# Attention on one core: six plain score units beside an off-diagonal group of steps, eleven beside a diagonal one, in place of eight beside each

## The chip, the cores and the metric

The kernel runs on one core of a Trainium2 chip. The metric is the device time of one execution in microseconds (us). Three executions of the kernel before took 1801.23, 1802.53 and 1802.96 us; their median, 1802.53 us, is the time before.

## The reference, cut to what matters

The input is 2048 tokens of 512 numbers. The layer adds three things: the input, a causal attention with 16 heads of 32, and a feed-forward of 4096 columns.

```
xn = layernorm(x)
q, k, v = split(xn @ w_qkv.T)             # 16 heads of 32
scores = where(causal, q @ k.T / sqrt(32), lowest)
probs  = softmax(scores)
attn   = (probs @ v) @ w_o.T
inter  = gelu_tanh(xn @ Wg.T) * (xn @ Wu.T)
out    = x + attn + inter @ Wd.T
```

The change touches only the attention. For a softmax in full precision each row's true maximum is subtracted, so the scores are computed twice: once plainly, to find the maxima, and once transposed, with the maximum folded into the matmul, for the exponentials.

## The kernel before, in words

`attention` works on eight pairs of heads. For each pair there are two streams.

**Steps.** A step is a chunk of 512 query columns against 128 keys, for both heads. Chunk qc has 4*qc + 4 steps, 40 in a pair. Four steps form a group (`GS = 4`): ten groups to a pair, 80 in all, of which groups 0, 2, 5 and 9 of each pair are diagonal (`DIAG`: the keys cross the causal border, and the steps are 512, 384, 256 and 128 columns wide), and groups 1, 3, 4, 6, 7 and 8 are off-diagonal. In the text k0 to k9 are these ten groups of a pair.

**Units.** A unit is one plain score matmul of 128 queries by up to 512 keys for one head (L1012, on TensorE), and the maximum of its rows by VectorE: `unit_max`, at L901, or at L897 where a part of the 512 is masked. A pair has 80 units (`NU`), 48 of full width at L901 and 32 masked ones at L897, eight each of 128, 256, 384 and 512 columns. They are numbered through all pairs, `NUNIT` = 640, and run about 58 units ahead of the steps; within a pair the narrow masked ones stand at 0 to 5, 10, 11, 14, 15, 18, 19, 28, 29, 34, 35, 40, 41, 54, 55, 62, 63, 70 and 71. When a row block is complete, VectorE joins its maxima (`join_parts`), GpSimd splits them in three bf16 parts (`split`, listed by `BATCHES`), TensorE turns them (`turn_max`, L1022, listed by `TURNS`), and ScalarE copies them beside the queries (`max_row`).

**How a group runs.** In its loop over k, TensorE issues the transposed scores of the next group's four steps (`scores_t`, L1040, eight matmuls; with `mask_t`, L1049, where the next group is diagonal). Seven eighths of the group's units stand between them (`some_units(0..6, 8)`). Then come the turns, the product with V of group k (L1066), row sums (L1083), and the last eighth of the units (`some_units(7, 8)`), called the tail below. TensorE takes all this in order. ScalarE computes the exponentials of the transposed scores (L818). They have three banks of PSUM (`ST_BUFS = 3`), so that `scores_t(x)` waits until the exponential of x-3 has been read. Plain units and turns share four banks (`S_BUFS = 4`), in the order of the list `ring`: `bank_free` makes a unit wait until VectorE has done what stood four places before it.

**Sums.** The exponentials are added up ahead of the row sums. GpSimd does most adds (L736): four of full width in an off-diagonal group, two each of 384, 256 and 128 columns in a diagonal one. In an off-diagonal group VectorE then adds the two sums of each head (`join_sums`, L956, two adds of 128x512), just before the group's last unit. `row_sums` of an off-diagonal group is run by TensorE in the next group. Only the groups without units give VectorE other adds.

**How many units a group has.** `unit_end` gives where group k's units end: eight more than the group before, until 640 are used up, which is in k2 of the last pair. `units_of(k)` is read by TensorE and VectorE alike. `BATCHES` follows from it; `TURNS` follows from the steps alone.

GpSimd's order in iteration k is: last adds of group k, first two adds of group k+1, the splits of `BATCHES[k]`, and in k3, k4, k6 and k7 of all but the first pair one product of the pair before with its reciprocal sums (`normalise`, L769).

Of the kernel before, what the change touches and what calls it, by code (L numbers as in the profile page):

```python
# [57 lines left out]
def values(nc, out, tt, xn_hi, xn_lo, wv_hi, wv_lo):  # L58

    t = slice(tt * P, (tt + 1) * P)  # L60
    for kt in range(KT):
        last = mm3(nc, out, xn_hi[:, kt, t], xn_lo[:, kt, t], wv_hi[:, kt, :], wv_lo[:, kt, :], kt == 0, kt == KT - 1)
    return last
# [285 lines left out]
def attention(nc, qk_scratch, v_scratch, sum_scratch, rsum_scratch, wo_t, wo_sb, attn_t, xn_hi, xn_lo, e_sb, wv_hi, wv_lo, p_v,  # L349
# [9 lines left out]
    GS = 4  # L359
# [2 lines left out]
    ST_BUFS = 3  # L362
    E_BUFS = 16
    S_BUFS = 4
    UNITS_GROUP = 8
    UNITS_FIRST = (20, 12)
    UNITS_AHEAD = 48
    TURN_LEAD = 1
# [5 lines left out]
    NS = len(STEPS)  # L374
# [5 lines left out]
    DIAG = [kt >= 4 * qc for qc, kt, _ in STEPS]  # L380
# [6 lines left out]
    NUNIT = PAIRS * NU  # L387
# [2 lines left out]

    BEHIND_V = {v: 5 for v in range(5, TT - 1)}
    FIRST_V = sum(BEHIND_V.values())
    TURNS_AT = TT - 3
    FIRST = FIRST_V + LEAD * 2
    unit_end, done = [], FIRST
    for k in range(NG):
        done = min(NUNIT, max(done + UNITS_GROUP, min(done + UNITS_FIRST[min(k, 1)], UNITS_GROUP * (k + 1) + UNITS_AHEAD)))
        unit_end.append(done)  # L400

    def units_of(k):
        return list(range(unit_end[k - 1] if k else FIRST, unit_end[k]))

# [3 lines left out]
    for p in range(PAIRS):  # L408
        for r in range(TC):
            last = p * NU + UNITS_TO[r]  # L410
            BATCHES[-1 if last <= FIRST else next(k for k in range(NG) if unit_end[k] >= last)].append((p, r))
            wanted = (p * NS + CHUNK_START[r] - LEAD) // GS
# [6 lines left out]

    BEFORE_TURNS = sum(count for v, count in BEHIND_V.items() if v < TURNS_AT)  # L420
    ring = list(range(BEFORE_TURNS)) + TURNS[-1] + list(range(BEFORE_TURNS, FIRST))
    for k in range(NG):
# [37 lines left out]
    with ExitStack() as ctx:  # L460
# [97 lines left out]
        def bank_st(x):  # L558
            return p_v[:, x % ST_BUFS, :] if x % ST_BUFS < V_FIRST else p_st3[:, :]
# [325 lines left out]
        def _(dve):  # L885
# [3 lines left out]
            def unit_max(n):  # L889
                a, i, b, w = UNITS[n % NU]  # L890
                part = max_part[:, a, i, b:b + 1]
                dve.wait_ge(scored, n + 1)
                if b == i // 4:
                    m = MASKED_UNITS.index(n)
                    if m >= 2:
                        dve.wait_ge(maxed, MASKED_UNITS[m - 2] + 1)
                    nc.vector.tensor_tensor_reduce(out=masked_scores[:, m % 2, 0:w], in0=p_s[:, slot[n] % S_BUFS, 0:w],  # L897
                                                   in1=score_mask[:, W - w:], scale=1.0, scalar=NO_MAX, op0=ALU.add,
                                                   op1=ALU.max, accum_out=part).then_inc(maxed, 1)
                else:  # L900
                    nc.vector.reduce_max(part, p_s[:, slot[n] % S_BUFS, 0:w], AX.X).then_inc(maxed, 1)  # L901
# [56 lines left out]

            for n in range(FIRST):
                unit_max(n)  # L960
# [33 lines left out]
        def _(pe):  # L994
# [8 lines left out]
            def scores(n):  # L1003

                p, u = divmod(n, NU)
                a, i, b, w = UNITS[u]
                if p == 0 and u < 2:
                    pe.wait_ge(first_loaded[a], 96)
                elif u < 2 if p else u in (SECOND, SECOND + 1):
                    pe.wait_ge(qk_loaded[p % PB][a], 96 * (p // PB + 1))  # L1010
                bank_free(slot[n])
                nc.tensor.matmul(p_s[:, slot[n] % S_BUFS, 0:w], q_stack[p % PB][a][0:ROWS, i * P:(i + 1) * P],  # L1012
                                 k_stack[p % PB][a][0:ROWS, b * W:b * W + w], start=True, stop=True
                                 ).then_inc(scored, 1)
# [109 lines left out]
            for v in range(V_FIRST, TT):  # L1124
# [6 lines left out]
                values(nc, bank_st(v), v, xn_hi, xn_lo, wv_hi, wv_lo).then_inc(v_projected, 1)  # L1131
                for _ in range(BEHIND_V.get(v, 0)):
                    scores(n)
# [442 lines left out]
def layer(nc, x, x_t, wqkv_t, wo_t, gate_p, up_p, gate_up_s, down_p, down_s, out_t):  # L1576
# [5 lines left out]
    with (nc.sbuf_tensor("xn_hi", [P, KT, S], F32R) as xn_hi, ExitStack() as ctx_wo):  # L1582
# [9 lines left out]
        with nc.psum_tensor("p_v", [P, V_FIRST, W], F32) as p_v, nc.semaphore("v_projected") as v_projected, \  # L1592
                ExitStack() as ctx_late:
            norm_and_project(nc, x, wqkv_t, qk_scratch, xn_lo_scratch, xn_hi, xn_lo, wv_hi, wv_lo, p_v, v_projected)
            wo_sb = ctx_wo.enter_context(nc.sbuf_tensor("wo_sb", [P, KT, H], F32))

            stack_hi = ctx_late.enter_context(nc.sbuf_tensor("stack_hi", [P, S], F32R))
            stack_lo = ctx_late.enter_context(nc.sbuf_tensor("stack_lo", [P, S], F32R))  # L1600
            rsum_rows = ctx_late.enter_context(nc.sbuf_tensor("rsum_rows", [P, S], F32))
            v_stack0 = ctx_late.enter_context(nc.sbuf_tensor("v_stack0", [P, 2 * W], F32))
            p_s = ctx_late.enter_context(nc.psum_tensor("p_s", [P, KT, W], F32))
            xt_first = ctx_late.enter_context(nc.semaphore("xt_loaded1"))
            loaded_first = ctx_late.enter_context(nc.semaphore("ffn_loaded0"))
            packed_first = rsum_rows[:, 0:3 * W].bitcast(I32).rearrange("p (m n) -> p m n", m=3)
            scales_first = (v_stack0[:, :].rearrange("p (m n) -> p m n", m=2), rsum_rows[:, 3 * W:])

            def load_first_chunk(sp):
                load_chunk(sp, 0, packed_first, *scales_first, gate_p, up_p, gate_up_s, down_p, down_s, loaded_first)  # L1610

            attention(nc, qk_scratch, v_scratch, sum_scratch, rsum_scratch, wo_t, wo_sb, acc, xn_hi, xn_lo, e_sb, wv_hi,
                      wv_lo, p_v, v_projected, p_s, stack_hi, stack_lo, rsum_rows, v_stack0, x_t, xt_first,
                      load_first_chunk)
            project_and_feed_forward(nc, x_t, xn_lo_scratch, gate_p, up_p, gate_up_s, down_p, down_s, xn_hi, xn_lo,
                                     wo_sb, stack_hi, stack_lo, packed_first, scales_first, p_v, p_s, xt_first,
                                     loaded_first, acc, out_t)
# [39 lines left out]
```

## Time and profile before

| | us |
|---|---|
| median of the three runs | 1802.53 |
| the profiled execution | 1800.53 |
| its span, first to last instruction | 1798.7 |
| TensorE (PE) busy in the span | 1762.1 |
| VectorE (DVE) busy | 1240.9 |
| ScalarE (ACT) busy | 715.9 |
| GpSimd (POOL) busy | 770.1 |

The attention lasts from about 150 us to about 720 us of the span, the projections stand before it, and the feed-forward behind it. In the profile an engine is busy from the start of an instruction to its end; a matmul's end is modelled, and a matmul on a pipelined engine overlaps the next, so spacing from start to start says more about TensorE than its busy time does. Times in the rows are counted from the span's start.

### The profile page before, as it was taken

Reading aid. Unit: us, or ns where it says so; the run is one execution under the profiler, and the core shown is the slowest. Engines: PE = TensorE matmul, PEld = TensorE weight load, DVE = VectorE, ACT = ScalarE, POOL = GpSimd, SP = SyncE. Lnnn points to the kernel's source line nnn. Section 1 sums busy time; section 2 is a strip of 40 time slices with the busy share of each in tenths; the row PEclk is TensorE's granted clock in tenths of the full one; section 3 lists DMA queues with packets and bytes.
Section 4 is the critical chain, followed back from the end, with each engine's and each line's share of the span. In section 5 each row is a group of like instructions: output and inputs, shape, how many; then the busy total and the mean of one; then the engine's idle time right before and its main releaser. Section 6 shows DMA issues by size and latency. Waiting matters only on the chain.

```text
span 1798.7 us, 28414 instructions
## 1 busy us (share of the span) xinstructions
PE 1762.1 (98%) x10176; PEld 1343.6 (75%) x10176; DVE 1240.9 (69%) x1834; ACT 715.9 (40%) x1171; POOL 770.1 (43%) x728
## 2 busy tenths in 40 slices
PE   7999999999999999999999999999999999999998
PEld 6886665555555656888888888888888888888887
DVE  5526888888888889686676567567567666666654
ACT  3323666666666665233223232323233223222322
POOL 1442889889889886122122222222222222222221
PEclk9999999999999999999999999999999999999999
DMA  8785053143143112511110110110110011010002
GB/s 286 218 239 147 10 105 83 29 105 77 35 105 72 40 40 60 182 29 36 35 35 0 35 35 0 35 35 0 35 35 13 22 35 28 7 35 0 1 1 94
DMA packets 75615, 108.55 MB, mean 60 GB/s; under 512 B 24912, under 2 KB 44992, under 8 KB 72384
## 3 DMA queue, kind: packets, MB, share of 16 engines
q1 hardware_dynamic: 75520, 107.34, 22.1%
q8 instruction: 53, 0.87, 0.2%
q14 instruction: 42, 0.34, 0.1%
HBM read 74.04 MB, written 29.59 MB: 58 GB/s over the span
## 4 chain that ended last, share of the span: by engine, by line
PE 59%; DVE 0%; ACT 0%; issue 0%; ACTq 0%
PE p_v L51 7%; PE p_up L50 7%; PE p_up L51 7%; PE p_v L50 7%; PE p_up L52 7%; PE p_v L52 7%; PE p_s L50 6%; PE p_s L51 6%; PE p_s L52 6%; PE p_s L345 0%; PE p_s L340 0%; PE p_s L339 0%; PE p_v L339 0%; PE p_up L340 0%; PE p_up L339 0%; PE p_v L340 0%
## 5 line engine op out<-in xcount | busy, mean ns | idle before, releaser
L1391 POOL TENSOR_SCALAR poly<-poly 128x1024 f32<-128x1024 f32 (+1 forms) x65 | 72.1, 1110 | 801.2 <-ACT poly L1348 801.2
L736 POOL TENSOR_TENSOR e_sum<-e_sb 128x512 f32<-128x512 f32 (+1 forms) x244 | 306.2, 1279 | 57.1 <-ACT e_sb L818 37.3
L901 DVE TENSOR_REDUCE max_part<-p_s 128x1 f32<-128x512 f32 x384 | 247.0, 683 | 61.2 <-PE p_s L1012 60.2
L818 ACT ACTIVATE e_sb<-p_v 128x512 f32<-128x512 f32 (+3 forms) x427 | 216.2, 548 | 119.6 <-PE p_v L1040 59.6
L1454 DVE SCALAR_TENSOR_TENSOR inter<-inter,gate 128x1024 f32<-128x1024 f32 (+1 forms) x65 | 78.6, 1209 | 241.1 <-ACT inter L1354 240.3
L50 PE MATMUL p_v<-xn_hi,w_hi 128*128 128x512 f32 x512 | 199.2, 389 | 0.0
L51 PE MATMUL p_v<-xn_lo,w_hi 128*128 128x512 f32 x512 | 199.2, 389 | 0.0
L52 PE MATMUL p_v<-xn_hi,w_lo 128*128 128x512 f32 x512 | 199.2, 389 | 0.0
L50 PE MATMUL p_up<-xn_hi,w_hi 128*128 128x512 f32 x512 | 199.2, 389 | 0.0
L51 PE MATMUL p_up<-xn_lo,w_hi 128*128 128x512 f32 x512 | 199.2, 389 | 0.0
L52 PE MATMUL p_up<-xn_hi,w_lo 128*128 128x512 f32 x512 | 199.2, 389 | 0.0
L1347 ACT ACTIVATE gate<-p_v 128x1024 f32<-128x1024 f32 (+1 forms) x65 | 65.9, 1015 | 333.2 <-PE p_v L52 333.2
L50 PE MATMUL p_s<-stack_hi,w_hi 128*128 128x512 f32 x504 | 196.1, 389 | 0.0
L51 PE MATMUL p_s<-stack_lo,w_hi 128*128 128x512 f32 x504 | 196.1, 389 | 0.0
L52 PE MATMUL p_s<-stack_hi,w_lo 128*128 128x512 f32 x504 | 196.1, 389 | 0.0
L1394 POOL TENSOR_TENSOR poly<-poly,gate 128x1024 f32<-128x1024 f32 (+1 forms) x65 | 179.4, 2759 | 5.4
L1354 ACT ACTIVATE inter<-poly 128x1024 f32<-128x1024 f32 (+1 forms) x65 | 68.0, 1047 | 202.0 <-POOL poly L1394 202.0
L1066 PE MATMUL p_o<-e_sb,v_stack 128*32 128x256 f32 (+1 forms) x2304 | 147.8, 371 | 0.0
L1474 DVE TENSOR_TENSOR acc<-acc,p_s 128x2048 f32<-128x2048 f32 x63 | 143.7, 2281 | 3.3 <-PE p_s L52 3.3
L818 ACT ACTIVATE e_sb<-p_st 128x512 f32<-128x512 f32 (+2 forms) x213 | 117.2, 550 | 60.6 <-PE p_st L1040 32.1
L897 DVE CUSTOM_DVE_ANT_0 recip<-p_s,score_mask 128x128 bf16<-128x128 f32 (+3 forms) x256 | 115.7, 485 | 36.9 <-PE p_s L1012 36.5
L1359 ACT ACTIVATE stack_hi<-inter 128x1024 fp32r<-128x1024 f32 (+1 forms) x65 | 68.1, 1048 | 163.0 <-DVE inter L1460 163.0
(190 smaller groups left out, 3502.5 us busy)
## 6 DMA issues: line engine op xcount, KB each, us to landing
k_stack<-qk_scratch SPq DMA_DIRECT2D x42, 256.0 KB, 7.5
qk_scratch<-out_hi SPq DMA_DIRECT2D x32, 256.0 KB, 2.6
qk_scratch<-out_lo SPq DMA_DIRECT2D x32, 256.0 KB, 3.3
q_stack<-qk_scratch SPq DMA_DIRECT2D x24, 256.0 KB, 6.4
xn_lo_scratch<-xn_lo SPq DMA_DIRECT2D x4, 1024.0 KB, 5.2
v_stack<-in_gate_up_s SPq DMA_DIRECT2D x64, 64.0 KB, 2.4
xn_lo<-xn_lo_scratch SPq DMA_DIRECT2D x4, 1024.0 KB, 14.0
scales<-in_gate_up_s SPq DMA_DIRECT2D x64, 64.0 KB, 2.5
```

What stands on the lines that cost most here:

```text
L50: nc.tensor.matmul(out, w_hi, x_hi, start=first, stop=False)
L51: nc.tensor.matmul(out, w_hi, x_lo, start=False, stop=False)
L52: return nc.tensor.matmul(out, w_lo, x_hi, start=False, stop=last)
L736: nc.gpsimd.tensor_tensor(*operands(k, i), ALU.add).then_inc(pool_summed, 1)
L818: nc.scalar.activation(e_sb[:, x % E_BUFS, 0:w], bank_st(x)[:, 0:w], ACT.Exp, scale=SCALE).then_inc(exp_done, 1)
L897: nc.vector.tensor_tensor_reduce(out=masked_scores[:, m % 2, 0:w], in0=p_s[:, slot[n] % S_BUFS, 0:w], in1=score_mask[:, W - w:], scale=1.0 ...
L901: nc.vector.reduce_max(part, p_s[:, slot[n] % S_BUFS, 0:w], AX.X).then_inc(maxed, 1)
L1066: last = nc.tensor.matmul(p_o[(2 * a + h) * D:(2 * a + h + 1) * D, 0, first - h * HALF:], v_stack[p % PB][:, kt, a, :], e_sb[:, (g * PIECE ...
L1391: nc.gpsimd.tensor_scalar(part_of(poly, h, parts), part_of(poly, h, parts), GELU_A, 1.0, ALU.mult, ALU.add).then_inc(poly_done, 1)
L1394: nc.gpsimd.tensor_tensor(part_of(poly, h, parts), part_of(poly, h, parts), part_of(gate, h, parts), ALU.mult).then_inc(poly_done, 1)
L1454: nc.vector.scalar_tensor_tensor(part_of(inter, h, parts), part_of(inter, h, parts), 1.0, part_of(gate, h, parts), ALU.add, ALU.mult).then ...
L1474: nc.vector.tensor_tensor(here, here, p_out[:, :, :], ALU.add).then_inc(added, 1)
```

## The change: what it does

Off-diagonal groups get six units each. Diagonal ones get what is left of 80 per pair: (8*10 - 6*6) // 4 = 11. The number of units, their order, all other work and the first lead of 58 units are as before. The end of the list is reached in k2 of the last pair again (with five units there, not six). By `unit_end` the split of each pair's third row block moves from k8 to k9 in `BATCHES`, in all pairs but the first block made ahead; its turn stays where it was.

With eleven units, nine stand among the transposed scores and two in the tail; with six it is five and one; with eight it was seven and one. For a pair in the steady state the units are now: k0 58 to 68, k1 69 to 74, k2 75 to 79 and 0 to 5, k3 6 to 11, k4 12 to 17, k5 18 to 28, k6 29 to 34, k7 35 to 40, k8 41 to 46, k9 47 to 57. Before they were k0 58 to 65, k1 66 to 73, k2 74 to 79, 0 and 1, k3 2 to 9, and so on by eights.

```diff
-    UNITS_GROUP = 8
+    UNITS_PAIR = 8
+    UNITS_JOINED = 6
...
+    DIAG_GROUPS = sum(DIAG[s] for s in range(0, NS, GS))
+    UNITS_DIAG = (UNITS_PAIR * NS // GS - UNITS_JOINED * (NS // GS - DIAG_GROUPS)) // DIAG_GROUPS
+
+    def units_beside(k):
+        return UNITS_DIAG if DIAG[GS * k % NS] else UNITS_JOINED
+
     unit_end, done = [], FIRST
     for k in range(NG):
-        done = min(NUNIT, max(done + UNITS_GROUP, min(done + UNITS_FIRST[min(k, 1)], UNITS_GROUP * (k + 1) + UNITS_AHEAD)))
+        done = min(NUNIT, max(done + units_beside(k), min(done + UNITS_FIRST[min(k, 1)], UNITS_PAIR * (k + 1) + UNITS_AHEAD)))
         unit_end.append(done)
```

## Rows read from the trace of the kernel before

**Rows 1.** The page's head and its first part.

```profile
span 1798.7 us, 28414 instructions
...
PE 1762.1 (98%) x10176; PEld 1343.6 (75%) x10176; DVE 1240.9 (69%) x1834; ACT 715.9 (40%) x1171; POOL 770.1 (43%) x728
```

**Rows 2.** Windows: stretch, length, busy PE, PEld, DVE, ACT, POOL; clock, DMA share, GB/s.

```profile
380.00:448.00 68.00, 65.94 (x593) 40.51 (x593) 58.27 (x130) 43.09 (x93) 60.22 (x73) 1.00 0.34 72
```

**Rows 3.** Waits, 205 to 650 us: total, times, longest.

```profile
PEld p_s L1012 <- DVE max_part L901: 8.8, 19, 0.8
```

**Rows 4.** Timeline of PE, products' beginnings: start, duration, engine, line, operation, tiles, shape, count.

```profile
373.45 0.64 PE L1083 MATMUL p_o<-e_sum,ones 128*32 128x256 f32 x8
...
380.26 1.29 PE L1066 MATMUL p_o<-e_sb,v_stack 128*32 128x256 f32 x18
...
387.35 1.93 PE L1066 MATMUL p_o<-e_sb,v_stack 128*32 128x256 f32 x32
...
393.23 0.64 PE L1083 MATMUL p_o<-e_sum,ones 128*32 128x256 f32 x8
...
399.92 1.93 PE L1066 MATMUL p_o<-e_sb,v_stack 128*32 128x256 f32 x32
...
406.54 0.64 PE L1083 MATMUL p_o<-e_sum,ones 128*32 128x256 f32 x8
...
412.83 0.64 PE L1083 MATMUL p_o<-e_sum,ones 128*32 128x256 f32 x8
...
419.65 1.93 PE L1066 MATMUL p_o<-e_sb,v_stack 128*32 128x256 f32 x32
...
426.28 0.64 PE L1083 MATMUL p_o<-e_sum,ones 128*32 128x256 f32 x8
...
434.32 0.64 PE L1083 MATMUL p_o<-e_sum,ones 128*32 128x256 f32 x8
...
441.59 0.64 PE L1083 MATMUL p_o<-e_sum,ones 128*32 128x256 f32 x8
```

**Rows 5.** Timeline of PE: k0's tail unit's start, and k2's last unit.

```profile
375.97 0.50 PE L1012 MATMUL p_s<-k_stack,q_stack 96*128 96x512 f32 x1
...
377.00 0.63 PE L1012 MATMUL p_s<-k_stack,q_stack 96*128 96x512 f32 x2
...
392.71 0.30 PE L1012 MATMUL p_s<-k_stack,stack_hi 96*128 96x128 f32 x1
```

**Rows 6.** Timeline of DVE: four maxima in a row in k2.

```profile
390.68 2.48 DVE L901 TENSOR_REDUCE max_part<-p_s 128x1 f32<-128x512 f32 x4
```

**Rows 7.** Timeline of ACT in k5: exponentials back to back.

```profile
411.06 1.10 ACT L818 ACTIVATE e_sb<-p_v 128x512 f32<-128x512 f32 x2
412.01 0.64 ACT L818 ACTIVATE e_sb<-p_st 128x512 f32<-128x512 f32 x1
```

**Rows 8.** Timeline of PE, first pair: products of k6 and k7.

```profile
216.47 1.93 PE L1066 MATMUL p_o<-e_sb,v_stack 128*32 128x256 f32 x32
...
222.27 0.64 PE L1083 MATMUL p_o<-e_sum,ones 128*32 128x256 f32 x8
```

**Rows 9.** Timeline of DVE: the two joins of k3, k6, k7 and k8.

```profile
400.82 1.32 DVE L956 TENSOR_TENSOR e_sum<-e_sum 128x512 f32<-128x512 f32 x2
...
420.32 3.42 DVE L956 TENSOR_TENSOR e_sum<-e_sum 128x512 f32<-128x512 f32 x2
...
427.81 3.18 DVE L956 TENSOR_TENSOR e_sum<-e_sum 128x512 f32<-128x512 f32 x2
...
435.81 2.33 DVE L956 TENSOR_TENSOR e_sum<-e_sum 128x512 f32<-128x512 f32 x2
438.07 3.07 DVE L901 TENSOR_REDUCE max_part<-p_s 128x1 f32<-128x512 f32 x5
```

**Rows 10.** Timeline of POOL: first adds of k5, last adds of k8.

```profile
407.38 2.73 POOL L736 TENSOR_TENSOR e_sum<-e_sb 128x384 f32<-128x384 f32 x2 [0.28 <-PE p_o L1083]
...
432.26 2.50 POOL L736 TENSOR_TENSOR e_sum<-e_sb 128x512 f32<-128x512 f32 x2
```

## The prediction

> **What bounds the kernel now.** I read the page's head and engine shares first: TensorE is busy 98% of the span, VectorE 69%, GpSimd 43% [rows 1]. These are means over stages, and the change lies in one. The windows of that stage come next: in 68 us of it TensorE is busy 65.94, GpSimd 60.22, VectorE 58.27, ScalarE 43.09 [rows 2]. Three engines are nearly full, so small waits on any of them count. The view of waits lists units that waited for VectorE's maxima, 19 times and 8.8 us in 445 [rows 3]; it counts only idle time, and matmuls overlap. So I measure the groups by the starts of their products [rows 4]. From one to the next, k0 to k9 take 6.81, 7.09, 5.88, 6.69, 6.62, 6.29, 6.82, 6.63, 8.04 and 7.27 us, 68.14 for a pair. k7 and k8 are the swollen ones.
>
> Four things set a group's length. (a) TensorE's columns: two full units, started at 377.00, take 0.63 together [rows 5], about 0.4 of it the last one's own length, so 0.24 from start to start in a stream. (b) ScalarE: exponentials follow at (412.01 - 411.06) / 2 = 0.48 [rows 7], and with three banks eight of them hold the transposed scores apart for about 3.0 us, 3.5 where ScalarE also copies out a chunk (k0, k1, k3, k6). (c) VectorE: full maxima follow at 0.60 (2.48 for four in [rows 6], 3.07 for five in [rows 9]), and a unit may start only when the maximum four before it is done. (d) GpSimd, whose adds the joins wait for.
>
> **What the change adds and removes.** No instruction is added or dropped: 80 units a pair before and after. Columns, maxima and adds cost the same in sum. Only places change, and (b), (c) and (d) decide what each place costs. I go through one steady pair, in the clock of [rows 4].
>
> *k0, nine units in the phase and k9's two in the tail ahead (before: seven and one).* The tail starts at 375.97 [rows 5], its first maximum about 0.5 later. Unit 66 waits for the maximum of 62, which is the seventh: 376.5 + 6 x 0.60 + 0.35 (256 columns; an estimate from half a full one, and a start) = 380.45. Units 64 and 65 are held likewise. After 66 come one transposed score and the product, 0.6, and the restarts after waits add some: 381.3 for 380.26, so +1.1. By columns alone three more units less the 0.4 that ScalarE already holds would be +0.3. I take +1.1, since 0.60 against 0.24 is measured.
>
> *k2, likewise.* VectorE starts four maxima at 390.68 [rows 6], and here they are 75 to 78. With 79 the last of them is done at 390.68 + 5 x 0.60 = 393.7. Unit 83 waits for 79; before, the phase's last unit started at 392.71 [rows 5]. So +1.0; by columns alone +0.1, as the added units are the narrow 0 to 3.
>
> *k5.* Two more full units: +0.5 by columns. VectorE holds the last at the same time, no more.
>
> *k1, k3, k4, k6, five units in the phase.* Here TensorE waits for ScalarE anyway: k3 and k6 have the copy, k1 and k4 have masks and exponentials in a chain. Two units less free almost nothing, and in k1, k3 and k6 the tail ahead has one more. I take -0.2, +0.2, -0.1, +0.1. Between nothing hidden and all: each from -0.5 to +0.25.
>
> *k7, k8.* Here units waited for VectorE, which was late with joins and maxima. With six units that goes: k7 falls from 6.63 to ScalarE's pace, 5.5 (-1.1). The first pair shows the size: its k7 takes 222.27 - 216.47 = 5.80 [rows 8]. k8 loses about 1.0, down to its chain with ScalarE. What is late next is the join.
>
> *k9, where I expect the loss.* VectorE joins k8 before k8's tail unit 46, and only then comes to k9's. The join needs GpSimd's last add of k8. GpSimd starts k5's adds when the row sums of k3 are through (407.38, it waited for PE) and then hardly stops until 432.26 + 2.50 = 434.76 [rows 10]. Before, the join started at 435.81 [rows 9], 1.0 later, so it was VectorE that was late. Now VectorE is early and GpSimd decides: the join can come at most 1.0 earlier. It then meets GpSimd's adds of k9 back to back. Two joins took 1.32 in k3, where they met none of the full adds, 2.33 in k8, 3.18 and 3.42 in k7 and k6 [rows 9]; I take 3.1. Gain in the start and loss in length nearly cancel (VectorE free at about 437.9, before 438.07). After it the turn of k9 waits for the maximum of the place four ahead: before that was unit 53, five maxima, 3.0 us; now it is 52 behind 46, 47 (and a row join), 48 to 52: seven, 4.4 us. So k9's product comes 1.2 to 1.3 later on GpSimd's clock than before. GpSimd's clock itself runs from k4's product, which k0 to k4 have moved by 1.1 - 0.2 + 1.0 + 0.2 - 0.1 = +2.0. Hence the end of k9 at about +3.0 to +3.3, I take +3.0; what k7 and k8 gave is taken back, and k9 grows from 7.27 to 9.8 (its own units alone would make it +0.3).
>
> **A rule weighed.** The joins' lengths in [rows 9] go with what GpSimd does beside them. The Trainium skill ("SBUF — State Buffer", section "Who interferes with whom") says that a VectorE instruction with two SBUF inputs and a GpSimd instruction that reads SBUF exclude each other for a whole instruction. The trace agrees: each of two joins meeting full adds comes to some 1.7 us, not 0.65. Without such exclusion a pair's k9 would be 1.8 us shorter, and the sum below some 11 us less.
>
> **The sum.** k0 +1.1, k1 -0.2, k2 +1.0, k3 +0.2, k4 -0.1, k5 +0.5, k6 +0.1, k7 -1.1, k8 -1.0, k9 +2.5: +3.0 a pair. Six pairs (the second to the seventh): +18.0. In the first pair GpSimd has no products of a pair before, and the joins are less late (k7 in [rows 8]); I take +1.6, between +0.5 and +3. In the last pair only k0 to k2 have units: k0 +1.1, k1 -0.2, k2 -0.2 (five units for six), +0.7; behind them everything is moved and nothing else. Sum +20.3. Split (p, 2), moved on GpSimd's queue past the last adds of k9 and the first two of k0, is wanted by a turn two groups after its old place; it costs 1.8 us of GpSimd behind the adds instead of ahead of them, and nobody waits (bounds 0 and 0.3 a pair). Everything outside the attention is untouched. No DMA is added or moved, save that those behind a late group are late with it.
>
> The profiled execution took 1800.53, 1.8 around its span of 1798.7, and lies 2.0 under the median. 1800.53 + 20.3 = 1820.8, on the median's footing 1822.8: I forecast 1823. Its own range is 1814 to 1830: k0 and k2 together between +1.2 and +2.4, k9 between +1.7 and +3.2 a pair.
>
> **The rivals.**
>
> *A. Slower, but little (1805 to 1812).* VectorE holds k0 and k2 as above, and the joins do not bind: GpSimd's adds come earlier, or the joins miss them (1.32 rather than 3.1). Then k9 is +0.3 in place of +2.5, the pair +0.8, the whole about +6: 1808. For it: GpSimd has some 8 us of idle time in 68 [rows 2]. Against it: that idle time lies in k0 to k2, not behind 407.38 [rows 10].
>
> *B. Faster.* The diagonal groups have no join to do, so VectorE takes the eleven maxima as they come, and only columns count there. Then k0 is +0.3, k2 +0.1, k5 +0.4, k9 +0.3; the off-diagonal ones -0.0, +0.1, -0.2, -0.1, -1.1, -1.0. That is -1.2 a pair, -8.5 in seven: 1794. It decides from the point at which VectorE gives a bank back within some 0.47 us a unit beside transposed scores; at 0.60 it loses. For it: k8's join is 1.0 behind GpSimd now, and VectorE's idle time before, some 10 us in 68 [rows 2], has to be somewhere. Against it: the idle time lies in the product phases, which nine units in a row cannot reach over four banks.
>
> *C. Nothing.* TensorE's 65.94 of 68 [rows 2] is the bound, the columns are the same, and what one group gains the next gives back: 1802.5. In the Trainium skill ("Perfetto Trace Analysis", section "Identifying the Most-Contended Engine") the most occupied engine is the one to look at, but matmul busy share is called a poor measure of it. Here that engine's groups of like work differ (k7 5.80 in the first pair, 6.63 later [rows 4, 8]), so busy TensorE is not full TensorE.
>
> *D. Slower still.* The late joins also delay the row sums, and exponentials wait for banks of e_sb: another 1 to 2 us a pair, 1831 to 1838.
>
> **How the numbers follow.** Forecast 0.50, A 0.16, B 0.17, C 0.10, D 0.07. Faster by over 0.2% (3.6 us, about what can be told from no change here): B, 0.17. Slower: 0.50 + 0.16 + 0.07 and half a case of C's edge, 0.74. Same: 0.09. The range goes from 1799, which leaves out most of B, to 1831, which leaves out most of D: about 0.8 inside. The groups' terms are sums of small waits, so I take more doubt into the range than [rows 4], with its repeating pattern, would suggest.
>
> **What would show it.** The starts of products in a steady pair: k0 and k2 each about 1 us longer, with waits of plain units on the maxima of L901 and L897 there, none in k7; k7 at about 5.5; joins of k7 and k8 starting within 0.1 us of the end of GpSimd's adds and taking about 3 us each pair; the turn of k9 waiting on L901, and k9 near 9.8. Wait time under [rows 3]'s line would grow to several times 8.8. If k0 stays under 7.2, the bank rule is wrong and B or C holds. If k0 and k2 grow and k9 stays near 7.6, it is A. Pairs of about 71.1 us confirm the sum, 67 refute it.

## The result, and the profile after

The changed kernel takes 1828.86 us (median of four runs, 1827.99 to 1830.31), the kernel before in the same runs 1801.88. The ratio is 1.0149, interval 1.0137 to 1.0161: 27 us slower. The forecast was 1823, range 1799 to 1831. The profiled execution took 1828.3 us.

The page's head and first part, for [rows 1], and one 72 us stretch by windows, for [rows 2] (same columns):

```profile
span 1826.5 us, 28414 instructions
...
PE 1774.4 (97%) x10176; PEld 1346.1 (74%) x10176; DVE 1247.3 (68%) x1834; ACT 718.2 (39%) x1171; POOL 765.4 (42%) x728
```

```profile
385.00:457.00 72.00, 68.05 (x600) 41.15 (x603) 59.62 (x131) 43.53 (x93) 59.88 (x74) 1.00 0.33 69
```

The counts are those of before, and VectorE's, ScalarE's and GpSimd's sums are within 1%. The work is the same and stands further apart: a pair needs some 72 us for it. TensorE's busy time even grew by 12 us, although it has no more to do; its share alone would not show the loss.

The timeline of PE for one steady pair, at the products' beginnings, answers to [rows 4]:

```profile
385.21 0.64 PE L1091 MATMUL p_o<-e_sum,ones 128*32 128x256 f32 x8
...
393.14 1.29 PE L1074 MATMUL p_o<-e_sb,v_stack 128*32 128x256 f32 x18
...
400.45 1.93 PE L1074 MATMUL p_o<-e_sb,v_stack 128*32 128x256 f32 x32
...
407.49 0.64 PE L1091 MATMUL p_o<-e_sum,ones 128*32 128x256 f32 x8
...
414.42 1.93 PE L1074 MATMUL p_o<-e_sb,v_stack 128*32 128x256 f32 x32
...
420.93 0.64 PE L1091 MATMUL p_o<-e_sum,ones 128*32 128x256 f32 x8
...
428.21 0.64 PE L1091 MATMUL p_o<-e_sum,ones 128*32 128x256 f32 x8
...
435.13 1.93 PE L1074 MATMUL p_o<-e_sb,v_stack 128*32 128x256 f32 x32
...
440.69 0.64 PE L1091 MATMUL p_o<-e_sum,ones 128*32 128x256 f32 x8
...
447.69 0.64 PE L1091 MATMUL p_o<-e_sum,ones 128*32 128x256 f32 x8
...
456.88 0.64 PE L1091 MATMUL p_o<-e_sum,ones 128*32 128x256 f32 x8
```

The table has the lengths from product to product, here and in the experiments, as means of the third to the sixth pair (us; "first" is the first pair, from its k0 to the next k0; "pair" the mean of the six after it). The names are those of the experiments below: half for cheaper maxima, k0_k1 for one part of the change, norm, prod, late and later for GpSimd's products elsewhere or shortened, split for the second join moved, mix for units by place; "before" or "after" says which kernel was edited. In the rows with a star, groups and pairs in which the granted clock fell are left out, and split_after's k0 and pair are of one pair alone; more on that behind the table.

| | k0 | k1 | k2 | k3 | k4 | k5 | k6 | k7 | k8 | k9 | pair | first |
|---|---|---|---|---|---|---|---|---|---|---|---|---|
| before | 6.82 | 7.09 | 5.87 | 6.69 | 6.62 | 6.29 | 6.82 | 6.63 | 8.05 | 7.27 | 68.14 | 66.95 |
| forecast | 7.9 | 6.9 | 6.9 | 6.9 | 6.5 | 6.8 | 6.9 | 5.5 | 7.0 | 9.8 | 71.1 | |
| after | 7.92 | 7.31 | 7.04 | 6.93 | 6.51 | 7.28 | 6.92 | 5.56 | 7.00 | 9.20 | 71.66 | 70.55 |
| half_before | 6.82 | 7.09 | 5.73 | 6.69 | 6.63 | 6.29 | 6.81 | 5.95 | 7.95 | 7.09 | 67.05 | 65.98 |
| half_after* | 7.05 | 7.31 | 6.30 | 6.94 | 6.51 | 6.75 | 6.93 | 5.55 | 7.00 | 8.64 | 68.96 | 67.54 |
| k0_k1* | 7.66 | 7.29 | 5.87 | 6.69 | 6.63 | 6.29 | 6.81 | 6.66 | 8.06 | 7.27 | 69.24 | 67.96 |
| norm_after | 7.92 | 7.29 | 7.04 | 6.94 | 6.50 | 7.29 | 6.93 | 5.86 | 7.00 | 8.70 | 71.49 | 70.55 |
| prod_after | 7.92 | 7.29 | 7.04 | 6.93 | 6.51 | 7.28 | 6.92 | 5.55 | 6.99 | 8.08 | 70.52 | 70.50 |
| split_before* | 6.81 | 7.10 | 6.49 | 6.69 | 6.67 | 7.21 | 6.82 | 6.30 | 7.20 or 8.33 | 7.27 | 69.10 | 67.53 |
| split_after* | 7.91 | 7.30 | 7.64 | 6.93 | 6.51 | 8.26 | 6.91 | 5.56 | 6.99 | 8.68 | 72.69 | |
| mix | 7.04 | 7.32 | 5.88 | 6.69 | 7.30 | 6.82 | 6.93 | 5.55 | 7.80 | 7.42 | 68.77 | 67.00 |
| late_before | 6.82 | 7.10 | 5.98 | 6.69 | 6.63 | 6.30 | 6.81 | 6.62 | 7.70 | 7.27 | 67.91 | 66.93 |
| later_before | 6.82 | 7.09 | 6.00 | 6.68 | 6.63 | 6.30 | 6.82 | 5.80 | 7.70 | 7.27 | 67.08 | 66.94 |
| later_after | 7.91 | 7.29 | 7.44 | 6.93 | 6.51 | 7.28 | 6.92 | 5.56 | 7.00 | 8.08 | 70.86 | 70.53 |
| later_7_9 | 7.05 | 7.10 | 6.00 | 6.69 | 6.63 | 6.30 | 6.82 | 5.81 | 7.10 | 7.27 | 66.83 | 66.60 |

In some of these traces TensorE's granted clock falls to half, from the upper level of 2.4 GHz to the lower of 1.2, for stretches of 3.4 us. One in the sixth pair of k0_k1 begins at 579.84; the windows show the time before it, the same place one pair earlier, and the stretch (columns as in [rows 2]):

```profile
506.75:510.55 3.80, 2.88 (x19) 1.85 (x18) 3.80 (x8) 2.38 (x7) 3.44 (x4) 1.00 0.00 0
576.00:579.80 3.80, 2.88 (x19) 1.85 (x18) 3.80 (x8) 2.34 (x7) 3.44 (x4) 1.00 0.00 0
579.90:583.20 3.30, 3.30 (x36) 1.53 (x37) 3.27 (x8) 1.18 (x2) 2.35 (x3) 0.50 0.99 231
```

TensorE did the same in both pairs, and only in one of them did the clock fall; k9 took 8.60 there and 7.27 in the others. Before has one such stretch, in the last pair at 678.23, where its k4 and k5 take 1.6 us more than in half_before, which has none there; after has none in the attention. So the lengths of before and after are not touched by it. half_after has two in a row in its sixth pair, split_before one each in two of its pairs, and split_after nine.

The span grew by 27.8: six pairs by 3.52 each, 21.1; the first by 3.6, and its first group, ahead of that, by 1.1; the last pair, up to the end of the attention, by 0.9 (before has its stretch of half clock there); and 1.1 had passed before the attention's first transposed score, where nothing is changed and single executions differ by a microsecond or two.

The waits from 205 to 650 us, by the same view as [rows 3], of maxima and joins; first the row of before for the masked maxima, which goes with [rows 3], then after:

```profile
PEld p_s L1012 <- DVE max_part L897: 6.4, 12, 0.9
```

```profile
DVE max_part L909 <- PE p_s L1020: 53.2, 67, 2.5
...
PEld p_s L1020 <- DVE max_part L909: 12.9, 38, 0.4
PEld p_s L1020 <- DVE max_part L905: 12.5, 24, 1.3
...
DVE e_sum L964 <- POOL e_sum L744: 2.3, 5, 0.5
```

Units wait for maxima of both lines for 25.4 us now and for 15.2 before. The line of [rows 3] alone went from 8.8 to 12.9, not to the several times 8.8 that was forecast as a sign; the masked maxima took the rest. The last row is new: the join (L956 before, L964 here) waits for GpSimd. And VectorE's queue beside it in k2 and at k6 to k8 (timeline of DVE; [rows 6] and [rows 9] before):

```profile
403.78 1.89 DVE L909 TENSOR_REDUCE max_part<-p_s 128x1 f32<-128x512 f32 x3
...
435.60 3.52 DVE L964 TENSOR_TENSOR e_sum<-e_sum 128x512 f32<-128x512 f32 x2
...
442.12 3.17 DVE L964 TENSOR_TENSOR e_sum<-e_sum 128x512 f32<-128x512 f32 x2
...
449.10 2.90 DVE L964 TENSOR_TENSOR e_sum<-e_sum 128x512 f32<-128x512 f32 x2 [0.47 <-POOL e_sum L744]
```

GpSimd's last two adds of k8 end at 446.56 + 2.51 = 449.07, 0.03 before k8's join, as forecast; k7's join starts 0.3 behind its adds (timeline of POOL, 446 to 449):

```profile
446.56 2.51 POOL L744 TENSOR_TENSOR e_sum<-e_sb 128x512 f32<-128x512 f32 x2
```

TensorE in k2: its narrow units 0 to 3 stop behind VectorE, one after another.

```profile
405.25 0.26 PE L1020 MATMUL p_s<-k_stack,stack_hi 96*128 96x128 f32 x1
405.81 0.30 PE L1020 MATMUL p_s<-k_stack,stack_lo 96*128 96x128 f32 x1 [0.30 <-DVE max_part L909]
406.33 0.39 PE L1020 MATMUL p_s<-k_stack,stack_hi 96*128 96x256 f32 x1 [0.21 <-DVE max_part L905]
```

### The profile page after: what moved, and what is told of

It reads as the page before. It is cut to its first block, busy times and chain, and to the rows that moved or that the text cites. A ratio compares the mean times of both kernels' runs of the same rounds, so it can differ in the third digit from the quotient of the medians.

```text
span 1826.5 us, 28414 instructions
## 1 busy us (share of the span) xinstructions
PE 1774.4 (97%) x10176; PEld 1346.1 (74%) x10176; DVE 1247.3 (68%) x1834; ACT 718.2 (39%) x1171; POOL 765.4 (42%) x728
## 4 chain that ended last, share of the span: by engine, by line
PE 58%; DVE 0%; ACT 0%; issue 0%; ACTq 0%
PE p_up L50 6%; PE p_v L50 6%; PE p_v L51 6%; PE p_up L51 6%; PE p_up L52 6%; PE p_v L52 6%; PE p_s L50 6%; PE p_s L51 6%; PE p_s L52 6%; PE p_s L345 0%; PE p_s L340 0%; PE p_s L339 0%; PE p_v L339 0%; PE p_up L339 0%; PE p_up L340 0%; PE p_v L340 0%
## 5 line engine op out<-in xcount | busy, mean ns | idle before, releaser
L744 POOL TENSOR_TENSOR e_sum<-e_sb 128x512 f32<-128x512 f32 (+1 forms) x244 | 302.5, 1263 | 89.7 <-ACT e_sb L826 71.4
L826 ACT ACTIVATE e_sb<-p_v 128x512 f32<-128x512 f32 (+3 forms) x427 | 216.5, 545 | 135.1 <-PE p_v L1048 71.1
```

The source lines that it names most:

```text
L744: nc.gpsimd.tensor_tensor(*operands(k, i), ALU.add).then_inc(pool_summed, 1)
L826: nc.scalar.activation(e_sb[:, x % E_BUFS, 0:w], bank_st(x)[:, 0:w], ACT.Exp, scale=SCALE).then_inc(exp_done, 1)
```

## The experiments

Two theories were to be told apart in each: that banks, VectorE's pace and GpSimd's lateness set the groups' lengths, or that columns and ScalarE do.

**Cheaper maxima, before and after.**

```diff
-                    nc.vector.reduce_max(part, p_s[:, slot[n] % S_BUFS, 0:w], AX.X)
+                    nc.vector.reduce_max(part, p_s[:, slot[n] % S_BUFS, 0:w // 2], AX.X)
-                                 scale=SCALE).then_inc(exp_done, 1)
+                                 scale=SCALE / 256).then_inc(exp_done, 1)
```

> Before, with the unmasked maxima (the L901 line) read over 256 of a unit's 512 columns and the exponentials' scale divided by 256; the output is not the layer's. A maximum then costs VectorE about 0.34 us in place of 0.60, 48 a pair. Bank theory (a unit waits for the maximum four places before): k7 and k8 lose their swelling, the pair falls from 68.1 to about 66, the whole by some 15 us to 1787. Rival (ScalarE and columns alone set the groups): within 3 us of before.

> After, with the same cut in the maxima and the exponentials' scale. Bank theory: k0, k2, k5 and k9 shrink to their columns; what is left against the half-maxima version of before is at most 1 us a pair, so at most 8 us and not 27, near 1792. Rival (eleven units are dear for their columns or their ScalarE chain, not for VectorE's maxima): still 20 to 27 us behind the half-maxima version of before.

1791.79 us before and 1809.94 after: 11 and 19 us less. The 27 between the two kernels became 18, not 8. By pairs it became 1.9 us from 3.5, so somewhat under half of the change's cost goes with the cheaper maxima; the 18 also hold stretches of half clock (mean granted clock 0.995 to 0.997 in the three executions after, 0.998 and 0.999 in the two before). k0 fell by 0.87, k2 by 0.74, k5 by 0.53: that was VectorE's pace. What remains over half_before in those three, 0.23, 0.57 and 0.46, stays when maxima are cheaper. But k9 fell only to 8.64 (half_before 7.09), and k8 of before hardly moved. The joins of k6, k7 and k8 in the half-maxima version of after show why, in the timeline of DVE:

```profile
422.25 3.02 DVE L964 TENSOR_TENSOR e_sum<-e_sum 128x512 f32<-128x512 f32 x2
429.11 3.45 DVE L964 TENSOR_TENSOR e_sum<-e_sum 128x512 f32<-128x512 f32 x2 [1.21 <-POOL e_sum L744]
436.36 2.90 DVE L964 TENSOR_TENSOR e_sum<-e_sum 128x512 f32<-128x512 f32 x2 [1.52 <-POOL e_sum L744]
```

A faster VectorE waits longer for GpSimd, and its joins still take turns with GpSimd's adds. The first pair, where GpSimd has no products, has k9 at 7.20. k7 of before fell from 6.63 to 5.95, although GpSimd's work was the same.

**One part alone.** Eleven units in k0, five in k1.

```diff
+    UNITS_AT = (11, 5, 8, 8, 8, 8, 8, 8, 8, 8)
-max(done + UNITS_GROUP, min(
+max(done + UNITS_AT[k % (NS // GS)], min(
```

> Before, with one part of the change alone: eleven units in k0 of each pair, five in k1, eight elsewhere. Bank theory: k0 +1.1 us as in after, k1 +0.2 (its second tail unit delays the transposed scores, and fewer units do not help there), so about +1.3 in each of eight pairs: +10 us. Rival (columns only): what k0 gets k1 gives back, 0 +/- 2 us.

1813.80 us, ratio 1.0053 (1.0037 to 1.0070), +11. k0 +0.84 and k1 +0.20, nothing elsewhere: 1.1 a pair, some 9 us in all. The rest is the clock: the trace has three stretches at half clock and took 1816.02; the execution with the highest mean clock, 0.999, took 1810.77. Fewer units in k1 give nothing back: shown.

**GpSimd's products elsewhere, after.** Moved from k3, k4, k6, k7 to k3, k4, k5, k9; then left in place over 32 columns.

```diff
-                if p > 0 and s in (12, 16, 24, 28):
+                if p > 0 and s in ((12, 16, 24, 28) if p == PAIRS - 1 else (12, 16, 20, 36)):
```

```diff
-                nc.gpsimd.tensor_tensor(here, here, rsum_rows[rows, qc * W:(qc + 1) * W],
+                nc.gpsimd.tensor_tensor(here[:, 0:32], here[:, 0:32], rsum_rows[rows, qc * W:qc * W + 32],
```

> After, with two of GpSimd's four products a pair moved out of k6 and k7 to k5 and k9 (all but the last pair). GpSimd theory (the join of k8 waits for its adds, and k9 pays): the adds of k7 and k8 end 1.5 to 3 us earlier, k9 falls from 9.2 to about 8.1 as it is in the first pair, -1.1 in six pairs: -6.6 us. Rival (k9 is long only because seven maxima stand before its turn): k9 stays at 9.2, 0 +/- 1.5 us.

> After, with each of GpSimd's products of a pair (28 of 128 heads' chunks, L777) over 32 columns in place of 512; the output is not the layer's. Moving two of them took only 0.5 us off k9. GpSimd theory: with some 1.1 us taken out of k3, k4, k6 and k7 each, its adds are early in every pair as they are in the first, the join of k8 waits for nothing, and k9 falls from 9.20 to 8.08 us, the first pair's: 6 x 1.1 = 6.7 us, near 1821. Rival (k9 differs from the first pair's for another reason, such as the previous pair's stores): k9 above 9.

norm_after: 1826.89, a miss. k9 fell by 0.5, and k7 grew by 0.3; the product in k5 stands before k6's last adds and keeps them late. prod_after: 1817.91, and k9 exactly 8.08, the first pair's. That is 11 us under after for 7 expected: the six pairs give 6.8, and most of the rest, 3.5, comes behind the last pair's k8, which is not explained. The joins of k6, k7 and k8 in prod_after:

```profile
432.95 1.48 DVE L964 TENSOR_TENSOR e_sum<-e_sum 128x512 f32<-128x512 f32 x2
...
438.81 2.37 DVE L964 TENSOR_TENSOR e_sum<-e_sum 128x512 f32<-128x512 f32 x2
...
445.47 2.11 DVE L964 TENSOR_TENSOR e_sum<-e_sum 128x512 f32<-128x512 f32 x2
```

5.96 us for the three, where after has 9.59: GpSimd is through with its adds or waits itself, and the joins meet fewer of them.

**The second join one unit into the next group.**

```diff
-                for n in units:
+                for i, n in enumerate(units):
+                    if i == 1:
+                        join_sums(k - 1, (1,))
                     if n == units[-1]:
-                        join_sums(k)
+                        join_sums(k, (0,))
                     unit_max(n)
```

> Before, with the join of the second head put one unit into the next group (two maxima now lie between the two joins of a group). Exclusion theory: a join waits for GpSimd's running add, and the maxima, which read PSUM alone, fill that wait, so VectorE gets 0.6 to 1.2 us back in each of k6, k7 and k8: k7 6.63 to 6.1, k8 8.05 to 7.3, k9 7.27 to 7.1, about -1.4 us a pair, -9 us. Rival (a join's length is its own, nothing is hidden): the work is the same, 0 +/- 2 us.

> After, with the second head's join put one unit into the next group in the same way. If the joins' lock and their late start make k9 what it is, k9 falls from 9.2 to about 8.2 and k5, whose first maxima stand behind k4's join, by 0.3: about -1.3 a pair, -9 us. Otherwise no change. k0 and k2, which have no join before them or a short one, stay at 7.9 and 7.0.

Both missed, with the wrong sign: split_before 1819.52 (1.0092, 1.0075 to 1.0108), split_after 1851.33 (1.0265, 1.0248 to 1.0282). In pairs at full clock each is 1.0 us a pair longer than its kernel without the edit, 69.10 for 68.14 and 72.69 for 71.66. Of split_after's 22 us over after, some 14 are the clock (an estimate: the six k0 and three k3 that a fall of the clock lengthens, each against the same group at full clock). split_before's trace is of its fastest execution, 1812.87 at a mean granted clock of 0.997; the other three took 1819 to 1821 at 0.995. k7 fell to 6.30 as expected, and k8 to 7.20 in two of the six pairs but rose to 8.3 or more in the others, which stays open. In the timeline of DVE of split_before, k4's joins:

```profile
410.87 0.69 DVE L956 TENSOR_TENSOR e_sum<-e_sum 128x512 f32<-128x512 f32 x1
412.86 0.69 DVE L901 TENSOR_REDUCE max_part<-p_s 128x1 f32<-128x512 f32 x1 [1.29 <-PE p_s L1014]
413.74 0.56 DVE L897 CUSTOM_DVE_ANT_0 recip<-p_s,score_mask 128x384 bf16<-128x384 f32 x1 [0.19 <-PE p_s L1014]
414.22 1.24 DVE L956 TENSOR_TENSOR e_sum<-e_sum 128x512 f32<-128x512 f32 x1
```

VectorE idles 1.29 in the product phase, where the join stood, and pays for it in the score phase, where the maxima pace TensorE: k2 +0.6, k5 +0.9. Here, what VectorE does during the product was nearly free, what it does beside units was not.

**Units by place.** `UNITS_AT = (9, 8, 8, 9, 8, 9, 7, 6, 7, 9)` on before.

> Before, with units by place: 9, 8, 8, 9, 8, 9, 7, 6, 7, 9 in k0 to k9. By the bank theory k7 falls to 5.6 (-1.0) and k8 to 7.3 (-0.7), while one more unit each in k0, k3, k5 and k9 costs 0.1, 0.2, 0.25 and 0.5: -0.6 a pair, about -4 us. If every unit moved out of a joined group is paid back in full by a diagonal one, as in after, it is above before by 2 to 6 us.

1805.90, ratio 1.0016 (1.0006 to 1.0026): a miss, 3 us above before where 4 below was expected. k7 gave its 1.1, but k4 took 0.7: nine units in k3 push its join to 2.4 us after the product begins, into k4's phase. k5 took 0.5. k1 took 0.23 with its eight units unchanged, behind a k0 with two tail units: so it is the second tail unit that lengthens k1, here and in after.

**GpSimd's products where it waits.** Four places a pair, over the pair's end; the last pair as before.

```diff
+            def products_at(p, kk):
+                here, after = (3, 9), (0, 1)          # late_before: (3, 4, 9), (0,)
+                return 0 < p < PAIRS - 1 and kk in here or p > 1 and kk in after
-                if p > 0 and s in (12, 16, 24, 28):
-                    normalise(p - 1, products % TC, splits,
+                if (p == PAIRS - 1 and s in (12, 16, 24, 28)) or products_at(p, s // GS):
+                    normalise(products // TC, products % TC, splits,
```

> Before, with GpSimd's four products a pair in k3, k4, k9 and the next pair's k0, in place of k3, k4, k6 and k7 (the last pair as before). GpSimd theory: the adds of k7 and k8 are early as in the first pair, where k7 and k8 take 5.80 and 7.67 us, not 6.63 and 8.05: 66.95 to 67.2 us a pair, -1.0 in six pairs, -6 us: 1796.5. Rival (in before VectorE's own lateness makes k7 and k8 long, and GpSimd only made after's k9): 0 +/- 2 us.

> Before, with the products in k3, k9 and the next pair's k0 and k1, where GpSimd waits most. GpSimd theory: the same as with k3, k4, k9 and k0, or up to 1 us a pair better as k5's adds are no longer behind a product: 1790 to 1797. Rival: 0 +/- 2 us.

> After, with the products in k3, k9 and the next pair's k0 and k1. With shortened products k9 fell from 9.20 to 8.08 and the pair to 70.52; here nothing is left out of the computation, and the GpSimd theory expects the same: 1819. What then remains above before (2.4 us a pair) is the banks' and VectorE's. Rival: k9 was helped by the shorter products themselves (fewer bytes), not by their absence before the adds: above 1825.

late_before: 1802.63, ratio 0.9994 (0.9985 to 1.0003), a miss; k8 falls to 7.70, k7 does not. later_before: 1795.48, ratio 0.9952 (0.9938 to 0.9965), faster than both kernels. later_after: 1821.76 (1.0100, 1.0084 to 1.0115), k9 at 8.08 again, with nothing left out; but k2 takes 0.40 more, since the exponentials wait for buffers that GpSimd's adds, now behind a product in k1, have yet to read:

```profile
404.26 1.19 ACT L830 ACTIVATE e_sb<-p_v 128x512 f32<-128x512 f32 x2 [1.08 <-POOL e_sum L744]
```

With the products moved in both kernels the change costs 26 us still (1821.76 against 1795.48), 3.8 a pair with that 0.40. GpSimd's lateness made k9 of after 1.1 longer, but it had made k7 and k8 of before 1.2 longer: it decides where the time is lost and adds next to nothing to the difference. The two versions of before differ by k4's product alone. Their joins of k6, k7 and k8, late_before first:

```profile
420.97 3.41 DVE L960 TENSOR_TENSOR e_sum<-e_sum 128x512 f32<-128x512 f32 x2
...
428.45 2.85 DVE L960 TENSOR_TENSOR e_sum<-e_sum 128x512 f32<-128x512 f32 x2
...
436.11 2.33 DVE L960 TENSOR_TENSOR e_sum<-e_sum 128x512 f32<-128x512 f32 x2
```

```profile
419.44 1.89 DVE L960 TENSOR_TENSOR e_sum<-e_sum 128x512 f32<-128x512 f32 x2
...
425.71 3.23 DVE L960 TENSOR_TENSOR e_sum<-e_sum 128x512 f32<-128x512 f32 x2
...
433.76 2.33 DVE L960 TENSOR_TENSOR e_sum<-e_sum 128x512 f32<-128x512 f32 x2
```

With k4's product in place GpSimd is still late at k6, its join takes 3.41 as before, and k7 pays 0.8.

**The best of both.** later_before with seven units in k8 and nine in k9.

> The version with GpSimd's products in k3, k9 and the next pair's k0 and k1, and one unit moved from k8 to k9 (seven and nine, eight elsewhere). In the first pair of the version with units by place, k8 took 7.00 with seven units and k9 7.24 with nine, where before has 7.67 and 7.24; its k0 took 7.04 behind a k9 with two tail units, not 6.82. So k8 -0.5, k9 0 to +0.2, k0 +0.2: -0.1 to -0.4 a pair, 1792 to 1795. Rival (any unit given to a diagonal group is paid there in full, as in after): k9 above 7.6 and the whole at 1797 or more.

1793.68 us, ratio 0.9954 (0.9939 to 0.9968). k8 7.10, k9 unchanged, k0 +0.2: -0.25 a pair in the profile, and -0.35 without the seventh, whose k2 takes 6.55. It beats before and after; that it beats later_before the intervals do not show.

## Why the prediction was right

The sign, the size and most places were right: 27 us for a forecast of 20, +3.52 a pair for +3.0.

- *k0 and k2, +1.1 and +1.0:* measured +1.10 and +1.17, and with cheaper maxima most of the first and over half of the second go. What stays of the first, 0.23, is what k9's second tail unit costs alone (k0 is 7.05 in later_7_9 too). VectorE's pace is shown; the number of banks was the same in all runs, so the part of the four banks rests on the kernel's order of waits. Of k2's remainder part is columns and masked maxima, which were not made cheaper.
- *k5, +0.5, "VectorE holds the last at the same time, no more":* this step failed. k5 grew by 0.99; 0.46 stays with cheaper maxima, 0.53 was VectorE's. Its first maximum stands behind the join of k4, and a join of row maxima (`join_parts`) among the last; I had counted neither as a delay, and no run separates the two.
- *k1, -0.2:* +0.2, the same with cheaper maxima. The sign was wrong. The second tail unit, shown by mix, moves the chain of transposed scores later, and fewer units give that chain nothing. k3, k4 and k6 came out at +0.24, -0.11 and +0.10, as forecast.
- *k7 and k8, -1.1 and -1.0:* measured -1.07 and -1.05. But the reason given, VectorE late by its own work, was half right. later_before takes no maximum away and has k7 at 5.80; half_before leaves GpSimd alone and has it at 5.95. So k7 was swollen by both together, and relief of either takes most of it away. k8 fell by 0.35 with the products moved and by a further 0.6 with one unit fewer (later_7_9); cheaper maxima take 0.1 from it in a steady pair and 0.64 in the first, where GpSimd has no products.
- *k9, +2.5:* +1.93. The mechanism is shown: the join of k8 waits for GpSimd (0.47 us in the row above), and with GpSimd's products away k9 is 8.08. So 1.1 of it is GpSimd's lateness, 0.8 the eleven units. The term was too big by 0.6, and that is k5's error on the other side: k4's product came 2.6 later (forecast 2.0) and k9's 3.5 (forecast 3.0), so the stretch between grew by 0.9 for a forecast 1.0, but k5 took 0.5 more of it. The joins took 2.90, not 3.1. The end of k9 followed GpSimd's order as forecast; its share of the pair came out smaller only because k5's came out larger.
- *The first pair, +1.6:* +4.7 with its first group, above its range of +0.5 to +3. Its k7 and k8, 5.80 and 7.67, had only 0.2 and 0.7 to give, while k0, k2 and k5 cost there what they cost elsewhere. I had credited it with the others' relief. This is 3.1 us of the sum's error. The six later pairs have as much, 21.1 for 18.0: k5 and k1 are 0.9 a pair, k2 0.2, and k9 takes 0.6 back.

The weight put on GpSimd was too great in one way. The prediction has the change lose its gain in k9 because GpSimd is late there; but before was held by the same lateness in k7 and k8, and with the products moved in both kernels the change costs as much. What costs is k0, k2, k5 and k9's own units, and they get back less from k7 and k8 then (0.9 a pair for 2.1).

Rival A is what k9's part would be without GpSimd, but prod_after shows that even then the pair stands at 70.52, 2.4 above before and not 0.8: A left out 0.5 each in k5 and k9 and 0.4 in k1. B's point of decision, 0.47 us a unit, was put to the test from the other side: half_after's maxima are faster than that, and k0 and k2 indeed fall to 0.2 and 0.4 to 0.6 above before. C is refuted by k0_k1, equal in columns and 1.1 us a pair slower at full clock. D did not show in after; later_after has its wait, 5.4 us in all.

The rule on exclusion (the Trainium skill, "SBUF — State Buffer", section "Who interferes with whom") agrees with the joins shown: 1.3 to 1.5 us for two without full adds beside them, 2.9 to 3.5 where both meet adds all along, and 1.9 to 2.4 where one of them meets only part of an add or none. split_before shows that it is not enough to know the exclusion: putting maxima between the joins cost more in k2 and k5 (1.5 together) than it won in k7 (0.3) and, in two pairs, in k8 (0.85).

## What to carry to other kernels

With few banks between two engines, count for each stretch the work of the slower engine, not its mean: here nine units in a phase cost 0.60 us each on VectorE against 0.24 on TensorE, and four banks cover no more. Balancing two engines by the number of units is not enough: the same units beside a phase that has no slack cost more than they free elsewhere, here 3.5 us a pair, and as much with GpSimd's products out of the way. The late third engine (GpSimd, 60 of 68 us) is a matter of its own: moving its deferrable work to where it waits won 7 to 9 us of 1802 in either kernel. Read a group's length pair by pair before taking a mean: one pair at half clock made k9 of k0_k1 look 0.33 longer, and it was not. And look for a stage that lacks one of the suspects, as the first pair lacks the products: its lengths are what the rest would take without it.

## What was not expected of the hardware

VectorE's join waits out GpSimd's running add even when it is issued at the moment at which the add before has ended. In half_before the joins of k6 and k7 started 0.03 us after the add that they waited for and took 3.46 us for two:

```profile
414.83 3.46 DVE L956 TENSOR_TENSOR e_sum<-e_sum 128x512 f32<-128x512 f32 x2
422.13 3.46 DVE L956 TENSOR_TENSOR e_sum<-e_sum 128x512 f32<-128x512 f32 x2 [1.02 <-POOL e_sum L736]
```

Before's joins in k3 took 1.32 [rows 9]. GpSimd's next add had already begun, so these joins, which waited for GpSimd, did not meet it free while it had more to do.

The clock is the other thing. In split_after it falls nine times to half for 3.4 us between 193 and 696 us, and each group hit takes 1.3 to 1.7 us longer (k0 7.91 at full clock, 9.20 to 9.63 otherwise); in after, which has the same matmuls, it does not fall in the attention at all. In k0_k1 what TensorE did before the fall does not tell that pair from the one ahead of it, so what decides it stays open.
